# Row maxima in packed banks, and a diagonal mask added by one matmul per bank

## What is computed

```python
qkv = clip(xn @ Wqkv.T, -8, 8); q, k, v = split(qkv)
q = layer_norm(q, q_ln_w, q_ln_b); k = layer_norm(k, k_ln_w, k_ln_b)   # then 32 heads of 16
scores = q @ k.T * 0.25 + slope[h] * (kpos - qpos)
scores = where(kpos <= qpos, scores, -1e30)
s = (softmax(scores) @ v) @ Wout.T
g = silu(ffn(xn))      # ffn: silu(gate) * up, then down; weights are dequantised from values 0 to 15
out = x + s * g
```

## Time and profile before

| | before |
|---|---|
| median of 3 runs | 1176.12 us (1174.08 to 1177.57) |
| profiled execution, its own time | 1172.21 us |
| its span | 1170.4 us |
| mean granted TensorE clock | 0.982 |
| TensorE matmul busy | 1090.4 us, 93% |
| TensorE weight load busy | 679.4 us, 58% |
| VectorE busy | 905.7 us, 77% |
| ScalarE busy | 632.1 us, 54% |
| GpSimd busy | 374.2 us, 32% |

### The profile page before, as it was taken

One profiled execution on the slowest core, in us unless ns is written; L12 is line 12 of the kernel. 1 busy time (PEld: TensorE's weight loads), 2 busy tenths in 40 slices (PEclk: granted clock), 3 DMA queues, 4 the chain that ended last, 5 costly groups with the idle time before them and its releaser, 6 DMA issues. The chain is left out here.

```text
span 1170.4 us, 23869 instructions
## 1 busy us (share of the span) xinstructions
PE 1090.4 (93%) x6401; PEld 679.4 (58%) x6401; DVE 905.7 (77%) x2115; ACT 632.1 (54%) x956; POOL 374.2 (32%) x472
## 2 busy tenths in 40 slices
PE   6999996999999999999999998899999999999996
PEld 4778771333333333333333433688788878887885
DVE  6888888788788888878888883677857876777776
ACT  3333330666667667666667667644544464445443
POOL 2666662121221212121221212134523443443343
PEclk9999995999999999999999999999999999999999
DMA  6335373334543434344443522100110020012000
GB/s 239 111 106 159 114 196 93 119 116 103 149 105 90 134 89 129 90 125 103 124 120 91 132 73 85 37 1 10 55 45 0 18 90 0 0 36 73 1 1 37
DMA packets 99725, 99.34 MB, mean 85 GB/s; under 512 B 28144, under 2 KB 80992, under 8 KB 99552
## 3 DMA queue, kind: packets, MB, share of 16 engines
q1 hardware_dynamic: 73216, 85.82, 25.4%
q10 hardware_dynamic: 26464, 12.98, 3.7%
HBM read 77.13 MB, written 21.23 MB: 84 GB/s over the span
## 5 line engine op out<-in xcount | busy, mean ns | idle before, releaser
L878 ACT ACTIVATE pr<-pair 128x1024 f32<-128x1024 f32 (+3 forms) x384 | 292.1, 811 | 157.9 <-PE pair L1001 101.4
L273 DVE CUSTOM_DVE_ANT_0 bank<-bank,sg 128x384 f32<-128x384 f32 (+3 forms) x512 | 241.5, 515 | 74.8 <-PE bank L283 70.4
L1281 DVE SCALAR_TENSOR_TENSOR gate<-pair,sgu,gate 128x512 f32<-128x512 f32 x168 | 126.1, 751 | 95.3 <-PE pair L1365 95.2
L1364 PE MATMUL pair<-xc_lo,w_gu 128*128 128x512 f32 x448 | 175.6, 392 | 1.8 <-DVE xc_lo L1264 1.8
L1365 PE MATMUL pair<-xc_hi,w_gu 128*128 128x512 f32 x448 | 174.8, 390 | 0.0
L276 DVE TENSOR_REDUCE mx<-bank 128x1 f32<-128x512 f32 x256 | 159.8, 682 | 7.4 <-PE bank L283 6.7
L1135 POOL TENSOR_TENSOR h_lo<-gate,h_hi 128x512 fp32r<-128x512 f32 x56 | 72.5, 1294 | 245.4 <-ACT h_hi L1160 245.4
L283 PE MATMUL bank<-xin_c,s_sb 108*128 108x512 bf16 (+3 forms) x384 | 116.7, 349 | 13.1 <-DVE mx L273 10.2
L1195 ACT ACTIVATE gate<-gate 128x512 f32<-128x512 f32 x56 | 35.5, 634 | 169.6 <-DVE gate L1281 169.6
L283 PE MATMUL bank<-ks,qs 108*128 108x512 bf16 (+3 forms) x384 | 109.0, 330 | 7.9 <-DVE mx L273 6.9
L996 PE MATMUL pair<-s_sb,xin_c 111*128 111x512 bf16 (+3 forms) x384 | 94.6, 330 | 8.8 <-DMA s_sb<-dt 4.1
(11 more groups left out here) (111 smaller groups left out, 1968.4 us busy)
## 6 DMA issues: line engine op xcount, KB each, us to landing
stk<-parts ACTq DMA_DIRECT2D x16, 768.0 KB, 5.0
zst<-in_z_all SPq DMA_DIRECT2D x24, 448.0 KB, 4.2
xin_c<-in_x SPq DMA_DIRECT2D x32, 256.0 KB, 2.7
sst<-in_w_all SPq DMA_DIRECT2D x16, 448.0 KB, 5.1
s_sb<-stk SPq DMA_DIRECT2D x96, 64.0 KB
xin_c<-stk SPq DMA_DIRECT2D x96, 64.0 KB
qs<-stk SPq DMA_DIRECT2D x96, 64.0 KB
ks<-stk SPq DMA_DIRECT2D x96, 64.0 KB
```

The costliest lines, as they stand in the source:

```text
L273: dve.tensor_tensor_reduce(out=src, in0=src, in1=tri[:, 512 - w:512], scale=1.0, scalar=-3.0e38, op0=ALU.add, op1=ALU.max, accum_out=dst). ...
L878: act.activation(pr[e % 3][:, 2 * p:2 * p + 2, 0:w], pair[p][:, :, 0:w], ACT.Exp, scale=SCALE)\
L1281: dve.scalar_tensor_tensor(out=a, in0=GB[j % 4], scalar=scale_of(n, k, it), in1=a, op0=ALU.mult, op1=ALU.add)\
L1364: pe.matmul(GB[j % 4], w, xc_lo[:, k, :], start=True, stop=False)
```

## The change

The triangle `tri` goes. The mask `behind` (128 x 128 bf16) is loaded early and lies, with the maxima, in the same buffer `sg0`. A piece is now `(qt, k0, w, j0, heads)`: it may hold several heads side by side in one bank. The 128 keys on the diagonal of a query tile form a piece of their own, with all four heads (512 columns). The keys ahead of them are cut in pieces of up to 512 keys; where 256 or fewer are left, two or four heads share a bank. A group then has 38 pieces (27 `EARLY`, 11 `LATE`) in place of 48. In a diagonal piece one matmul of 512 columns first writes the mask into all four heads' places, its moving operand being the 128 columns of `identb` repeated four times, and the four score matmuls add to it. Every maximum is a plain reduction that gives one value a head. Since a tile's maxima come in up to three parts, they are set to -3e38 once, and `negate` merges the parts and negates them in one instruction on VectorE, which `chain` on GpSimd did in part before. `D0` counts as two turns of the three banks (`D0_TURNS`), so that the number of turns stays a multiple of three. The head holds 5 pieces in place of 8, the tail 3 in place of 6, and 2 of them in place of 4 stand ahead of the last PV product.

```diff
-        def pieces(tiles):
-            return [(qt, j, k0, min(512, (qt + 1) * P - k0))
-                    for qt in tiles for j in range(GH) for k0 in range(0, (qt + 1) * P, 512)]
+        def pieces(qt):
+            out = [(qt, qt * P, P, 0, GH)]
+            for k0 in range(0, qt * P, 512):
+                w = min(512, qt * P - k0)
+                n = 1 if w > 256 else 512 // w
+                out += [(qt, k0, w, j0, n) for j0 in range(0, GH, n)]
+            return out
+        def columns(pc):
+            return pc[2] * pc[4] * (2 if pc[1] == pc[0] * P else 1)
...
-        HEAD = 8
-        LATER_KEYS = len(EARLY) // 2
+        HEAD = 5
+        LATER_KEYS = sum(pc[1] > 0 for pc in EARLY)
-        TAIL = 6
-        BEFORE = 4
+        TAIL = 3
+        BEFORE = 2
+        D0_TURNS = 2
...
             dve.wait_ge(m_full, n + 1)
-            if k0 + w == (qt + 1) * P:
-                apart(dve, "dve")
-                dve.tensor_tensor_reduce(out=src, in0=src, in1=tri[:, 512 - w:512], scale=1.0,
-                                         scalar=-3.0e38, op0=ALU.add, op1=ALU.max, accum_out=dst).then_inc(m_free, 1)
-            else:
-                dve.tensor_reduce(dst, src, AX.X, ALU.max).then_inc(m_free, 1)
+            dve.tensor_reduce(dst, b[:, 0:heads * w].rearrange("p (j c) -> p j c", c=w), AX.X, ALU.max).then_inc(m_free, 1)
...
-            pe.matmul(b[:, 0:w], qs[s][0:ROWS_MAX, qt // 4, j, (qt % 4) * P:(qt % 4 + 1) * P],
-                      ks[s][0:ROWS_MAX, j, k0:k0 + w], start=True, stop=True).then_inc(m_full, 1)
+            mask = k0 == qt * P
+            if mask:
+                pe.matmul(b[:, :], behind, identb[:, :].unsqueeze(1).to_broadcast([P, GH, P]), start=True, stop=False)
+            for j in range(heads):
+                mm = pe.matmul(b[:, j * w:(j + 1) * w], qs[s][0:ROWS_MAX, qt // 4, j0 + j, (qt % 4) * P:(qt % 4 + 1) * P],
+                               ks[s][0:ROWS_MAX, j0 + j, k0:k0 + w], start=not mask, stop=not mask or j == heads - 1)
+            mm.then_inc(m_full, 1)
-        def over_halves(dve, n):
+        def negate(dve, n, mx, dneg, done):
             dve.wait_ge(m_free, n)
-            dve.tensor_tensor(mx1[:, 0, :, :], mx1[:, 0, :, :], mx1[:, 1, :, :], ALU.max).then_inc(mx1_done, 1)
+            dve.tensor_reduce(dneg.rearrange("p (j t) -> p j t", j=GH), mx.rearrange("p c t j -> p j t c"),
+                              AX.X, ALU.max, negate=True).then_inc(done, 1)
...
-                            sp.dma_start(tri[:, :], tri_in).then_inc(tri_done, 16)
+                            sp.dma_start(behind, behind_in).then_inc(behind_in_sb, 16)
...
+                dve.memset(mx0, -3.0e38).then_inc(mx_set, 1)
+                dve.memset(mx1, -3.0e38).then_inc(mx_set, 1)
...
-                pool.wait_ge(mx1_done, 1)
-                chain(mx1[:, 0, :, :], 0)
+                pool.wait_ge(neg1_done, 1)
+                chain(dneg1, 0)
```

More of the change, by code:

```diff
@@ L85, in build @@
         sg0 = sb("sg0", [P, 512], F32)
-        tri = sg0
-        mx0 = sb("mx0", [P, GH, 4], F32)
-        mx1 = sb("mx1", [P, 2, GH, 4], F32)
+        mx0 = sg0[:, 0:32].rearrange("p (a t j) -> p a t j", a=2, t=4)
+        mx1 = sg0[:, 32:80].rearrange("p (a t j) -> p a t j", a=3, t=4)
+        dneg0, dneg1 = sg0[:, 80:96], sg0[:, 96:112]
+        behind = sg0[:, 128:192].bitcast(BF16)
         s_sb = sb("s_sb", [P, 4, 512], F32)
@@ L203, in build @@
         diag = [kt >= 4 * qb for qb, kt, _ in STEPS]
-        def pieces(tiles):
-            return [(qt, j, k0, min(512, (qt + 1) * P - k0))
-                    for qt in tiles for j in range(GH) for k0 in range(0, (qt + 1) * P, 512)]
-        EARLY = sorted(pieces(range(4, 8)), key=lambda pc: -pc[2])
-        LATE = pieces(range(4))
-        HEAD = 8
-        LATER_KEYS = len(EARLY) // 2
+        def pieces(qt):
[7 more added lines that the diff above has]
+            return pc[2] * pc[4] * (2 if pc[1] == pc[0] * P else 1)
+        EARLY = sorted(sum((pieces(qt) for qt in range(4, 8)), []), key=lambda pc: pc[1] == 0)
+        LATE = sum((pieces(qt) for qt in range(4)), [])
+        HEAD = 5
+        LATER_KEYS = sum(pc[1] > 0 for pc in EARLY)
         PLACES = 3 * NSTEP
@@ L229, in spread @@
             width = [w for e in range(NSTEP) for w in (512 - STEPS[e][2], 512 - STEPS[e][2], 512 - STEPS[e - 1][2])]
-            total, work = sum(width[lo:hi]), sum(pc[3] + 60 for pc in lot)
+            total, work = sum(width[lo:hi]), sum(columns(pc) + 60 for pc in lot)
             out, at, passed = {h: [] for h in range(PLACES)}, 0, 0
@@ L233, in spread @@
                 passed += width[h]
-                while at < len(lot) and (h == hi - 1 or sum(pc[3] + 60 for pc in lot[:at]) < work * passed / total):
+                while at < len(lot) and (h == hi - 1 or sum(columns(pc) + 60 for pc in lot[:at]) < work * passed / total):
                     out[h].append(lot[at])
@@ L250, in build, with numbered @@
         PREP = len(HEAD_ORDER)
-        number = ({x: n for n, x in enumerate(order)}, {x: n for n, x in enumerate(own)})
+        def numbered(work):
+            return {x: n + (D0_TURNS - 1 if "D0" in work[:n] else 0) for n, x in enumerate(work)}
+        number = (numbered(order), numbered(own))
         def at(x, last):
@@ L634, in _ @@
                 aggr(t, 1)
+                dve.wait_ge(mx_set, 2)
                 for n in range(FILL_A):
@@ L777, in half_job @@
                       .then_inc(z_in, 16)
-                sp.dma_start(behind[:, :], behind_in).then_inc(mask_in, 16)
                 for b in (1, 0):
@@ L933, in ring @@
                         if x == "D0":
-                            dve.wait_ge(m_full, base(i) + at(x, last) + 1)
+                            dve.wait_ge(m_full, base(i) + at(x, last) + D0_TURNS)
                             apart(dve, "dve")
-                            dve.tensor_copy(dt_sb[0][:, :], ring_bank(x, last)[0:48, 0:P // 2].bitcast(BF16)).then_inc(m_free, 1)
+                            dve.tensor_copy(dt_sb[0][:, :], ring_bank(x, last)[0:48, 0:P // 2].bitcast(BF16)).then_inc(m_free, D0_TURNS)
                         elif isinstance(x, str):
@@ L967, in ring @@
                             if x == "D0":
-                                trans_d(2 * i + 1, ring_bank(x, last), m_full)
+                                trans_d(2 * i + 1, ring_bank(x, last), m_full, D0_TURNS)
                             else:
@@ L1000, in second @@
                         for jj in range(2):
-                            mm = pe.matmul(pair[p][:, jj, 0:P], identb[:, :], behind[:, :], start=False, stop=True)
+                            mm = pe.matmul(pair[p][:, jj, 0:P], identb[:, :], behind, start=False, stop=True)
                     mm.then_inc(s_full[p], 1)
```

61 lines of the change are left out of this document (28 added, 33 removed).

## The result

| | before | after |
|---|---|---|
| median, range | 1175.68 us (1174.08 to 1177.57), 4 runs | 1190.25 us (1188.45 to 1190.82), 4 runs |
| profiled execution, its span | 1172.21, 1170.4 us | 1188.45, 1186.5 us |
| TensorE matmul, weight load busy | 1090.4, 679.4 us | 1104.2, 707.1 us |
| VectorE busy | 905.7 us | 873.3 us |
| mean granted clock | 0.982 | 0.984 |

The changed kernel is 1.2% slower: the ratio is 1.0121, 95% interval 1.0102 to 1.014. VectorE lost 32.4 us of work and the program became 14.6 us longer.

A forecast was written before the change was run, and what follows sets the result against it. TensorE was taken to bound the group loop, held in places by VectorE and ScalarE. Groups +2.7 and start -0.35 gave +2.3 us: 1174.5 on the profiled execution, 1178.4 on the median, range 1170 to 1190.

The forecast's parts named there:

- (1): Rival, chance 0.11: weight loads set the pace of narrow matmuls in packed four-head pieces; 21 us slower, 1199 us.
- (2): Rival, chance 0.07: a VectorE maximum over four rows pays 0.07 us per row; 14 us slower, 1192 us.
- (a): Step 1's second pair to step 5: four masks add 0.88 us, 1.24 of waits go; -0.36 us a group.
- (b): Start of a group: 0.22 us less TensorE work, but ScalarE sets both starts, so 0.
- (c): Steps 5 to 9: same plain maxima at the same places, VectorE slightly later; +0.05 us a group.
- (d): Step 9 to the group's end: three masks +0.66, moved columns +0.43, a 0.60 wait goes; +0.49 us.
- The groups together: Sum of the four places in the group loop: +0.18 us per group, +2.7 over 15 groups.
- The start: Ahead of the first group: VectorE's first maxima -1.1 us, the head pieces at the lower clock +0.75; -0.35 us.
- (3): Rival, chance 0.06: VectorE sets the pace of the whole group; 32 us faster, 1144 us.
- (4): Rival, chance 0.18: masks find more cover, group 0.29 us shorter, with the start -4.7 us; 1171 us.
- (5): Rival, chance 0.03: packing only moves the waits for VectorE to the next full bank; 30 us slower, 1206 us.

The follow-up runs named there:

- the run without the two extra causes: Changed kernel with 192 unused bytes behind sg0 and the idle turn moved from D0 to behind a step 0 piece: 1175.93 us, ratio 1.0006.
- the run with the idle turn in step 0: Changed kernel with the second turn moved from D0 to behind the group's second piece, plus 192 unused bytes behind sg0: 1175.93 us, ratio 1.0006.
- the shifted kernel before: Kernel before with 64 unused bytes behind sg0, so later buffers start 64 bytes past a multiple of 256: 1181.1 us, ratio 1.007.
- the pad: 192 unused bytes behind sg0, meant to restore the later buffers' earlier addresses; alone on the changed kernel: 1184.32 us, ratio 1.011.
- the split piece: Changed kernel with 192 bytes behind sg0, tile 5's four-head piece split into two of two heads, and D0 back to one turn: 1180.43 us, ratio 1.0036.
- the longer tail: Changed kernel with 192 bytes behind sg0, tile 5's four-head piece split, D0 one turn, and a tail of five pieces for three: 1166.1 us, ratio 0.9914.

## Why the prediction was off

Forecast was no change, 1178.4, with 0.51 on it; measured was 1190.25, a quarter of a microsecond past the range's upper end of 1190, 7 above the forecast's own range, and 14.6 above before. That it comes so near the range is luck: the upper end was drawn from rivals (1) and (2), which did not happen, and what carried the time there are two costs that no rival had. By its steps:

- **(a) steps 1 to 5**, forecast -0.36: measured -0.40. The waits of the earlier trace rows are gone, and the stretch takes 11.4 us as said.
- **(b) the start**, 0: measured 0 in step 0. The earlier trace rows have the same 3.01 us (381.32 to 384.33 in the changed kernel). ScalarE covers the mask there, as the run with doubled masks shows (1.81 in step 0 too).
- **(c) steps 5 to 9**, +0.05: **this step failed**, measured +0.55. It took maxima and places into account, not turns of the ring. That `D0` counts as two turns stands in the description of the change; the question that a turn without an item asks, who is now one item nearer to VectorE, was not put. With the idle turn elsewhere the term is 0.00 (9.88 us for steps 5 to 8, as in the kernel before).
- **(d) the tail**, +0.49: measured +0.53 with the turn elsewhere, +0.55 as changed. Three masks and the columns, less the wait ahead of the last piece of the earlier trace rows, as the sum had it.
- **The groups together**, +0.18: +0.14 in the run without the two extra causes. Times 15 that is 2.1, for 2.7 forecast. One reading was wrong without harm to it: the stretch of the earlier trace rows is not the whole loop, which goes on for another group, to the last exponentials at 728.57.
- **The start**, -0.35: measured -0.9 between the marks, VectorE's early maxima 2.1 us shorter where 1.1 were forecast, and the head longer, 3.50 us (203.22 to 206.72) for 2.67, +0.83 where 0.75 were forecast. From the transpose of the row maxima to the first exponential it is 5.86 us for 5.53, +0.33, which was not forecast.
- **Block 1: this step was not there at all.** The prediction let the change touch "this stage and the 26 us ahead of it". **This step failed too**: removing two small buffers moved all those behind them, +6.8 us.

The sum itself, +2.3 us, is within the interval of the run with the idle turn in step 0 (ratio 0.9991 to 1.002, which is -1.1 to +2.3 us, at its upper end). The two things left out cost the profiled execution 15 x 0.57 = 8.6 and 6.8 us.

The rivals: (1) is out. Here are TensorE's rows in the changed kernel, mask and narrow matmuls in turn:

```profile
355.79 0.39 PE L292 MATMUL bank<-ks,qs 108*128 108x128 bf16 x4
356.01 0.38 PE L290 MATMUL bank<-identb,sg 128*128 128x512 bf16 x1
356.23 0.39 PE L292 MATMUL bank<-ks,qs 108*128 108x128 bf16 x4
356.45 0.60 PE L1006 MATMUL pair<-s_sb,xin_c 111*128 111x512 bf16 x2
```

Four matmuls with four fresh loads take 0.22, 0.055 each, and their loads, which last 97 to 100 ns in the profile, keep up. The Trainium skill's TensorE: Matmul & The Clock Gate (section Back-to-back issue gap) gives 81 ns for a 128-column matmul in a stream with its loads; these rows have 55, and the measurement decides. (2) is out too, from the groups of VectorE's maxima (busy us, mean ns of one, idle before):

```profile
L280 DVE TENSOR_REDUCE sg<-bank 128x1 f32<-128x512 f32 x256 | 159.9, 682 | 14.4 <-PE bank L292 13.6
L280 DVE TENSOR_REDUCE sg<-bank 128x4 f32<-128x512 f32 x160 | 106.6, 686 | 50.8 <-PE bank L292 49.8
```

Four rows cost 4 ns more than one, not 0.2 us. (The rival counted thirty more row starts; with the four pieces of two heads it is 34.) (3) and (4) wanted shorter groups. (5), that the waits only move, had the right kind of event, a wait for VectorE at a full bank, but at one place (0.57 us) rather than everywhere (2.0), and from the turn rather than from the packing. What was lacking among the rivals was one on what the diff moves without naming it: addresses.

**What stays open** is what the addresses are worth in the whole time. In the profiles block 1's last copy begins at 174.1 to 176.3 us without an offset, and at 181.6 to 185.1 with one, 5 to 11 us apart. The runs say 8.5 for the shifted kernel before (ratio 1.0051 to 1.0089), of which some 1.5 are its longer groups. The changed kernel with the pad stands at 1.011, and without it at 1.0115 and 1.0121: by the medians only about 1 us. Two estimates by other pairs of runs, each against the kernel before on its own chip, lie between. From 1.0115, without edits, to 1.0006, with the pad and the idle turn in step 0, are 12.8 us, of which 15 x 0.56 = 8.4 are the groups; to 1.0036, with the pad and the split piece, are 9.3, of which 15 x 0.28 = 4.2. That leaves 4 to 5 us for the addresses. The feed-forward stage, 434.9 to 438.5 us in the profiles above with the same code and a granted clock from 1.00 to 0.98, scatters by nearly as much.

## What to carry to other kernels

When a change makes a ring's count fit by giving one item two turns, treat that turn as a lost buffer at that very place, and put it where another engine sets the pace anyway. When a change removes or adds a buffer, compare the addresses of all that are declared behind it before anything is said of the stages that it "doesn't touch", and try the buffers of large transfers at multiples of 256 bytes; offsets of 64 and 128 cost 5 us and more in block 1 here, other offsets and other stages were not tried. And work that costs TensorE its full price in a busy step is nearly free in a wait for another engine: the longer tail, which moves two masked pieces there, brought the kernel with the split piece from a ratio of 1.0036 to 0.9914, where the packing alone gained nothing.

## What the runs showed of the hardware

**A start address in SBUF off a multiple of 256 bytes slowed this kernel's DMA.** With `parts` and the buffers about it 64 or 128 bytes past a multiple of 256 the highest peak past the first slices of block 1's GB/s row is 287 to 296, where it is 347 to 364 without, and most stores of 768 KB land by turns after 4.5 and 6.6 us, not 4.0 and 5.6. Five kernels with an offset, of both designs, show the one, eight without show the other. The Trainium skill's DMA: Bandwidth & Descriptors (section How a descriptor splits into AXI transactions) says that a transaction must start at a multiple of 256 bytes, so that a descriptor that starts off one begins with a transaction from the boundary below, whose first bytes are fetched and not used. That an offset costs agrees with these traces; the skill gives no time for it, and that this is the cause of the slower stores no run shows.

**A moving operand that repeats 128 columns four times streams as fast as any other**: 0.22 us for the 512 columns of the mask (356.01 to 356.23), the same as for 512 different ones (377.65 to 377.87 in the earlier trace rows).
